# A fused scan and feed-forward kernel on one core: a fifth weight-ring entry, a transpose table, new step tables, and even pairs of row 0 summed on TensorE

## What is computed

```python
xx, res = split(x @ in_w.T, 2)                  # 512 inner channels each
xx = silu(conv4(xx) + conv_b)                   # causal, per channel
delta, B, C = split(xproj(xx), [16, 32])
delta = softplus(delta @ dt_w.T + dt_b)
for l in range(512):                            # 16 states per channel
    h = exp(delta[l] * A) * h + delta[l] * B[l] * xx[l]
    y[l] = sum over states of h * C[l]
y = (y + xx * D) * silu(res)
x = layernorm(x + y @ out_w.T)
h = silu(x @ w1.T * s1) * (x @ w2.T * s2)       # 1024 hidden
h = gelu(h @ h1.T * s); h = gelu(h @ h2.T * s)  # 1024 x 1024 each
out = layernorm(x + h @ w3.T * s3)
```

## Time and profile before

| | |
|---|---|
| median of 3 runs | 2764.91 us (2760.35 to 2766.14) |
| the profiled execution's own time | 2763.87 us |
| its span, first to last instruction | 2762.0 us |
| busy share of the span | PE 88%, DVE 86%, ACT 77%, POOL 62% |
| share of the 16 DMA engines' span, two main queues | 52.3% (GpSimd's), 33.5% (SP's) |
| mean granted TensorE clock | 0.947 |

### The profile page before, as it was taken

The page is one execution under the profiler, slowest core; times in us unless marked ns, Lnnn a source line. Parts: engine busy times, 40 slices in busy tenths (PEclk is TensorE's granted clock), DMA queues, the critical chain, the costliest instruction groups (busy, mean ns, idle before and its releaser), DMA issues. The chain is left out here.

```text
span 2762.0 us, 36137 instructions
## 1 busy us (share of the span) xinstructions
PE 2432.1 (88%) x12034; PEld 1844.0 (67%) x12034; DVE 2386.9 (86%) x2356; ACT 2114.3 (77%) x3225; POOL 1708.1 (62%) x1607
## 2 busy tenths in 40 slices
PE   5567998989899898989989899998989999898988
PEld 2335675767767576776757677675766767576767
DVE  6788899999999989999999999999898999989730
ACT  5676887969788796978879697887969789696711
POOL 1345666765665676566667656666765676666644
PEclk6568999999999999999999999999999999999999
DMA  5988898989989898998979889898988989898933
GB/s 164 312 207 192 204 227 197 241 194 219 219 207 229 194 241 200 216 221 206 229 194 239 201 214 219 206 228 195 241 203 211 216 208 226 203 232 204 252 95 118
DMA packets 226794, 581.64 MB, mean 211 GB/s; under 512 B 25920, under 2 KB 26304, under 8 KB 226128
## 3 DMA queue, kind: packets, MB, share of 16 engines
q0 software_dynamic: 73728, 268.47, 52.3%
q1 hardware_dynamic: 152880, 310.84, 33.5%
HBM read 301.86 MB, written 20.45 MB: 117 GB/s over the span
## 5 line engine op out<-in xcount | busy, mean ns | idle before, releaser
L767 DVE TENSOR_TENSOR_SCAN scan_ps<-dA,scan_ps 128x1024 f32<-128x1024 f32 x381 | 870.9, 2286 | 113.7 <-PE scan_ps L402 106.4
L626 ACT ACTIVATE dB<-duT,bT 128x512 f32<-128x512 f32 x1024 | 715.4, 712 | 115.5 <-PE scan_ps L402 115.5
L969 POOL DMA_DIRECT2D y<-hC x512 | 449.8, 879 | 543.4 <-DVE hC L778 382.6
L617 ACT ACTIVATE dA<-delta,a_neg 128x512 f32<-128x512 f32 (+1 forms) x1024 | 692.5, 711 | 3.1 <-DVE scan_ps L767 2.0
L402 PE MATMUL scan_ps<-ident,dB 128*128 128x128 f32 x4096 | 575.0, 287 | 130.6 <-DVE hC L778 107.5
L514 PE MATMUL ffn_ps<-hb_hi,ring 128*128 128x512 f32 x1536 | 649.7, 423 | 44.0 <-POOL hb_lo L1008 20.8
L402 PEld LDWEIGHTS scan_ps<-ident,dB 128*128 128x128 f32 x4096 | 500.1, 147 | 240.5 <-DVE hC L778 94.5
L514 PE MATMUL ffn_ps<-hb_lo,ring 128*128 128x512 f32 x1536 | 606.8, 395 | 0.0
L778 DVE TENSOR_TENSOR hC<-scan_ps,c_rows_sb 128x1024 f32<-128x1024 f32 x381 | 464.0, 1218 | 40.3 <-DMA c_rows_sb<-c_rows 11.0
L514 PE MATMUL ffn_ps<-ha_hi,ring 128*128 128x512 f32 x1024 | 437.8, 428 | 6.3 <-POOL ha_lo L1008 4.6
L961 POOL TENSOR_TENSOR hC<-hC,c_rows_sb 128x1024 f32<-128x1024 f32 x131 | 324.5, 2477 | 183.4 <-DVE hC L767 179.4
(11 more groups left out here) (99 smaller groups left out, 3168.5 us busy)
## 6 DMA issues: line engine op xcount, KB each, us to landing
y<-hC POOLq DMA_DIRECT2D x512, 512.0 KB, 6.0
ring<-rounded_weights SPq DMA_DIRECT2D x704, 256.0 KB, 4.1
c_rows_sb<-c_rows SPq DMA_DIRECT2D x256, 256.0 KB, 4.7
x<-ffn_w SPq DMA_DIRECT2D x22, 512.0 KB, 8.1
rounded_weights<-ffn_w SPq DMA_DIRECT2D x22, 512.0 KB, 10.3
xt<-x_chan SPq DMA_DIRECT2D x16, 512.0 KB, 4.2
xt<-x_tok SPq DMA_DIRECT2D x16, 512.0 KB, 4.4
out_st<-x_chan SPq DMA_DIRECT2D x16, 512.0 KB, 4.6
```

The source lines that it names most:

```text
L617: nc.scalar.activation(dA[:, s % DA_RING, s % 2:], delta2[:, par, c, s % 2:], ACT.Exp, scale=a_neg[:, c, n:n + 1]).then_inc(dA_ready, 1)
L626: nc.scalar.activation(dB[:, n % 2, t, :], duT[:, t, :], ACT.Copy, scale=bT2[:, par, t, n:n + 1]).then_inc(dB_ready, 1)
L767: nc.vector.tensor_tensor_scan(states, dA[:, a:a + 2, :].rearrange("p a l -> p (a l)"), b, 0.0, ALU.mult, ALU.add).then_inc(scan_done, 1)
L969: pool.dma_start(y2[:, par, c:c + 2, :], hC[:, slot], accum_op=ALU.add).then_inc(y_added[p % 2], 16)
```

## The change

- The ring has five entries, and an entry's place goes by its number over all rows (44 is no multiple of 5). To make room, small tables are computed in place of their inputs. The next row's first five entries are loaded in step 18, not four in step 14.
- `b_pair` goes by a table `B_AT`: within some steps of where it stood.
- Most step tables are laid anew. `POOL_PAIRS` has six pairs, not eight; `FIRST_POOL_PAIRS` (row 0) is as it was.
- Row 0 adds its 16 even pairs on TensorE (`sum_pair`: two products with the identity into `ffn_ps[1]` and `ffn_ps[2]`, which are free in iteration 0), and VectorE adds the two sums to `y2` in step 0 of iteration 1. Its 16 even transfers are gone.
- The DRAM copy of the weights is issued ten slots before row 0's scan and twelve during it, every fifth step.

```diff
-RING = 4
+RING = 5
-T_RES = (0, 4, 5, 8)
-T_GATE = (2, 5, 7, 11)
-T_OUT = (12, 13, 14, 17)
-T_ADD = (15, 18)
+T_RES = (0, 6, 7, 9)
+T_GATE = (2, 5, 8, 11)
+T_OUT = (12, 14, 16, 17)
+T_ADD = (16, 18)
-E_W3 = (10, 11, 13, 14)
-E_SCALE = (12, 17)
-E_ADD = (14, 19)
-E_STATS = (15, 21)
+E_W3 = (10, 11, 12, 18)
+E_SCALE = (12, 19)
+E_ADD = (14, 20)
+E_STATS = (17, 21)
-L1_AT = (22, 23, 24, 25, 26, 27, 28, 29)
-HALF_AT = (31, 32, 34, 35, 36, 38, 40, 41, 42, 43, 45, 46, 47, 48, 49, 50, 51, 52, 53, 54, 55, 57, 59, 60, 62,
-           63, 64, 65, 66, 68, 69, 71)
-GELU_AT = (38, 39, 39, 46, 46, 47, 50, 51, 55, 57, 57, 65, 66, 67, 71, 71)
+B_AT = (-2, 0, 4, 5, 7, 9, 10, 12, 14, 15, 18, 20, 22, 24, 26, 28, 31, 32, 34, 35, 37, 40, 42, 43, 47, 48, 50, 51,
+        54, 56, 58, 61)
+L1_AT = (22, 24, 25, 26, 27, 28, 29, 31)
+HALF_AT = (31, 32, 34, 35, 36, 37, 38, 40, 42, 44, 45, 46, 47, 48, 49, 50, 51, 52, 53, 54, 55, 56, 57, 60, 61, 62,
+           63, 64, 65, 70, 71, 72)
+GELU_AT = (38, 39, 39, 45, 46, 47, 49, 51, 56, 57, 57, 65, 65, 66, 72, 72)
-F_DT = (40, 41, 43, 44)
-F_PLUS = (45, 46, 48, 50)
-F_BASE = (40, 41, 43, 46)
-F_LOST = (46, 49, 51, 52)
-F_LN = 52
+F_DT = (40, 41, 43, 46)
+F_PLUS = (44, 46, 47, 49)
+F_BASE = (41, 43, 46, 50)
+F_LOST = (47, 47, 49, 51)
+F_LN = 51
-COPY_AT = tuple(range(6, 2 * SLOTS + 6, 2))
+COPY_AT = tuple(range(-26, -16)) + tuple(range(2, 62, 5))
+CLOSE_AT = 0
-POOL_PAIRS = (0, 8, 10, 12, 13, 16, 17, 28)
+POOL_PAIRS = (1, 8, 11, 13, 16, 17)
 FIRST_POOL_PAIRS = (0, 3, 4, 9, 14, 16, 17, 18, 25, 27, 28)
+SUM_AT = tuple(min(63, 2 * p + (5 if p in FIRST_POOL_PAIRS else 3)) for p in range(0, PAIRS, 2))
...
+            def sum_pair(p):
+                wait_product(pe, 0, p)
+                for c in range(2):
+                    mm = nc.tensor.matmul(ffn_ps[1 + c][:], ident[:], hC[:, p % HC_SLOTS, c, :],
+                                          start=(p == 0), stop=(p == PAIRS - 2))
+                mm.then_inc(y_summed, 1)
...
-                    if s % 2 == 0:
-                        if s // 2 + 1 < PAIRS:
-                            if scan is not None:
-                                b_pair(scan, s // 2 + 1)
-                        elif front is not None:
-                            b_pair(front, 0)
+                    if scan is not None and s in B_AT:
+                        b_pair(scan, B_AT.index(s))
+                    if front is not None and s - TILES in B_AT:
+                        b_pair(front, B_AT.index(s - TILES))
+                    if i == 0 and s in SUM_AT:
+                        sum_pair(2 * SUM_AT.index(s))
...
+                    if i == 1 and s == CLOSE_AT:
+                        dve.wait_ge(y_summed, PAIRS // 2)
+                        for c in range(2):
+                            nc.vector.tensor_tensor(y2[:, 0, c, :], ffn_ps[1 + c][:], y2[:, 0, c, :], ALU.add
+                                                    ).then_inc(y_closed, 1)
...
+                if on_pe(r, p):
+                    return
                 wait_product(pool, r, p)
```

More of the change, by code:

```diff
@@ L62 @@
 F_DBL_OUT = 40
-F_BT = 46
+F_BT = 48
 F_BT_OUT = 51
-F_DT = (40, 41, 43, 44)
-F_PLUS = (45, 46, 48, 50)
-F_BASE = (40, 41, 43, 46)
-F_LOST = (46, 49, 51, 52)
-F_LN = 52
+F_DT = (40, 41, 43, 46)
[3 more added lines that the diff above has]
+F_LN = 51
 F_DELTA = (53, 53, 53, 53)
 F_DELTA_U = (53, 53, 53, 53)
-F_Y = (55, 55, 58, 63)
-F_DU = (54, 55, 56, 58)
+F_Y = (59, 59, 61, 63)
+F_DU = (55, 56, 57, 58)
 F_XR = 51
@@ L104, in products_upto, with added_upto, on_pe @@
     return sum(on_pool(k // PAIRS, k % PAIRS) == pool for k in range(r * PAIRS + p))
+def added_upto(r, p, k):
+    return 16 * sum(q % 2 == k and not on_pe(row, q) for row in range(r + 1) for q in range(p if row == r else PAIRS))
+def on_pe(r, p):
+    return r == 0 and p % 2 == 0
 def build(nc, x, xT_in, in_wT, chan, xproj_wT, dt_wT, out_wT, ffn_w, ffn_s, w3_s, ident_in, out):
@@ L162, in build @@
         rstd = sb("rstd", [P, 2, TT])
+        conv_half, a_neg = ch[:, :, 0:TAPS + 1], ch[:, :, C_ALOG:]
+        s1_half, s12_half = fs[:, 0, :], fs[:, 1, :]
         xT_front = xt[:].rearrange("p (k t) d -> p k (t d)", k=KD)
@@ L262, in wait_slot @@
             g = r * PAIRS + p - HC_SLOTS
-            if g >= 0:
-                eng.wait_ge(y_added[g % 2], 16 * (g // 2 + 1))
+            if g >= 0 and on_pe(g // PAIRS, g % PAIRS):
+                eng.wait_ge(y_summed, g // 2 + 1)
+            elif g >= 0:
+                eng.wait_ge(y_added[g % 2], added_upto(g // PAIRS, g % PAIRS + 1, g % 2))
         def main_loop(eng, iteration, *args):
@@ L342, in load_weights @@
                         sp.wait_ge(pe_half, f * HALVES + (used - FIRST_HALF + 1))
-                    dst = ring[:, e % RING, :].bitcast(F32)
+                    g = f * ENTRIES + e
+                    dst = ring[:, g % RING, :].bitcast(F32)
                     src = w_dram[e // 2]
                     sp.dma_start(dst, src[:, (e % 2) * ENTRY_COLS:(e % 2 + 1) * ENTRY_COLS]
-                                 ).then_inc(ring_loaded[e % RING], 16)
+                                 ).then_inc(ring_loaded[g % RING], 16)
             def iteration(i, par):
@@ L351, in iteration @@
                 for s in range(TILES):
-                    if (s + 4) % DC == 0:
-                        n = (s + 4) // DC
+                    if (s + C_LEAD) % DC == 0:
+                        n = (s + C_LEAD) // DC
                         if n < STATES:
@@ L501, in wait_entry, with entry @@
             def wait_entry(f, e):
-                per_row = ENTRIES // RING
-                pe.wait_ge(ring_loaded[e % RING], f * (16 * per_row) + 16 * (e // RING + 1))
-            def entry(e):
-                return ring[:, e % RING, :]
+                g = f * ENTRIES + e
+                pe.wait_ge(ring_loaded[g % RING], 16 * (g // RING + 1))
+            def entry(f, e):
+                return ring[:, (f * ENTRIES + e) % RING, :]
             def products(dst, steps, first, last, full):
@@ L526, in l1_tile @@
                         pe.wait_ge(l1_x32 if prev % 2 else l1_gate, f * HC + (prev // 2 + 1))
-                    steps = [(entry(o)[:, (q * KD + k) * P:(q * KD + k + 1) * P], a[:, k, :])
+                    steps = [(entry(f, o)[:, (q * KD + k) * P:(q * KD + k + 1) * P], a[:, k, :])
                              for k in range(KD) for a in (x1T_hi, x1T_lo)]
@@ L545, in half_tile @@
                 wait_entry(f, e)
-                steps = [(entry(e)[:, k * P:(k + 1) * P], a[:, kh * HC // 2 + k, :])
+                steps = [(entry(f, e)[:, k * P:(k + 1) * P], a[:, kh * HC // 2 + k, :])
                          for k in range(HC // 2) for a in src]
@@ L560, in w3_tile @@
                         wait_entry(f, e)
-                    steps = [(a[:, 2 * q + k, t * P:(t + 1) * P], entry(e)[:, k * DIM:(k + 1) * DIM])
+                    steps = [(a[:, 2 * q + k, t * P:(t + 1) * P], entry(f, e)[:, k * DIM:(k + 1) * DIM])
                              for k in range(2) for a in (ha_hi, ha_lo)]
@@ L982, in gate_tile @@
                     for k in range(2):
-                        pool.wait_ge(y_added[k], r * (8 * PAIRS) + 8 * PAIRS)
+                        wait_past(pool, y_added[k], added_upto(r, PAIRS, k))
+                    if r == 0:
+                        pool.wait_ge(y_closed, 2)
                 pool.wait_ge(v_ready, r * DC + (c + 1))
```

32 lines of the change are left out of this document (15 added, 17 removed).

## The result

The changed kernel takes 2681.82 us (median of 4 runs, 2681.34 to 2685.69), the kernel before in the same series 2765.52 us. The ratio is 0.9701, interval 0.9685 to 0.9716: 3% faster. The profiled execution's span went from 2762.0 to 2679.5 us, 82.5 us less. 2714 us was predicted, with 2675 to 2762 as the range. The direction and the range held; the gain is 82.5 us in the span where 50.2 were summed.

What follows compares the result with a forecast made beforehand. A round was taken as a long part TensorE ends and a short one VectorE ends. Gains of 37.7 (13 rounds), 8 (row 0), 1.5 (row 1) and 3 (end), together 50.2 us, gave 2714 us, range 2675 to 2762.

Steps and rivals of the forecast that it cites:

- The serial piece: Half tiles reordered around step 39's `xproj` product: 2.2 us a round saved before scans 22 to 24, 0.3 wait at 21.
- Gate: Gates early in a round: 1.9 us tanh wait becomes 1.0, the next vanishes; 1.2 of waiting at pair 2's transposes.
- The end of the long part: Before pair 9's transposes: TensorE work moves to idle time, ending waits of 0.65 us before scan 9 and 0.7 for `hb_hi`.
- Products on VectorE: Two pairs' products a round move from GpSimd to VectorE: 2.4 us charged, bounds 1.2 to 2.4.
- The sum of a round: Steady round: 5.3 of 10.8 us of VectorE waits saved, 2.4 paid, 2.9 gained; 37.7 over 13 rounds.
- The ring: Ring entry loads held to step 18: no gain, no cost; if late, one landing (4 us) a round.
- Row 0: Sums replace 16 transfers: 12 us of transfer waits saved, 4 of new transpose waits, 8 gained (-3 to 14).
- Row 1, last row and drain: Row 1 gains 1.5 us after 1.4 for closing the sums; drain gains 2, the last row's scans 1.
- Transfers bind: Rival, chance 0.12: the stretch with transfer share 1.00 keeps its length, so 1.0 us a round gained; 2740 us.
- TensorE binds row 0: Rival, chance 0.12: at the lower clock the sums fill TensorE; row 0 loses 5 us instead of gaining 8; 2727 us.
- Nearly all waits go: Rival, chance 0.07: nearly all VectorE waits in a round vanish, 8.4 us a round gained; 2637 us.
- Slower: Rival, chance 0.11: saved waits return at the next transposes and two products lengthen VectorE's part, 34 us lost; 2787 us.

Runs made afterwards that it cites:

- The serial piece alone: Kernel before with five half tiles moved around the `xproj` and `dt` products as in the change, nothing else: 2775.30 us, ratio 1.0040.
- The late W3 tile alone: Kernel before with only the fourth `w3_tile` moved behind the output products (step 14 to 18, its scaling and addition later): 2748.88 us, ratio 0.9947.
- single products: Kernel before with one GpSimd product given to VectorE, in two runs: pair 28 2776.18 us (ratio 1.0047), pair 12 2778.77 us (1.0050).
- the old eight pairs: Changed kernel with GpSimd's products set back to pairs 0, 8, 10, 12, 13, 16, 17, 28: 2729.18 us, ratio 0.9876.
- the ring of four: Changed kernel with four ring entries in place of five, all else as changed: 2765.64 us, ratio 0.9997.

## Why the prediction was right, and where it was mis-sized

**What bounds the kernel: right in kind.** A round ends by hand-overs between TensorE and VectorE, and the waits of VectorE that the experiments on the order of work moved could be named. But the walk left out one side of these hand-overs, as the ring and the GpSimd pairs show.

**The serial piece: right.** Expected 1.5, 0, 1.5 and 0.3 us before scans 22, 23, 24 and 21; measured 1.51, none, 0.78, 0.44. The serial piece alone in the kernel before gave the first two and 2.56 at pair 24. So the other tables fill 1.8 us of that gap, which fits the 1.3 to 2.2 credited to `F_PLUS` and `F_LOST`; no run isolates these two.

**Gate: right in kind.** Expected 1.0 for tanh and 1.2 at pair 2; measured 0.9 and 0.8. The 0.9 are two waits, so the second one shrank and did not vanish.

**The end of the long part: right.** The wait before scan 9 and that for `hb_hi` are gone. The late W3 tile alone takes the first away, and leaves 0.6 us a round of the second.

**Products on VectorE: the pairs were taken for work alone.** 2.4 us were charged. In the kernel before, single products cost 0.8 and 1.1, so as a price of the work the charge was fair. In the changed kernel busy time rose by 1.8 a round, and the old eight pairs cost 3.3 us a round rather than saving 2.4. The step counted what VectorE has to do and did not walk what the choice sets for the transposes two pairs on: a pair on GpSimd frees its bank of `scan_ps` at the end of its scan, a pair on VectorE only at the end of its product. With pair 11 on GpSimd the transposes of pair 13 need not wait, and both runs that gave pair 11 back and pair 10 to GpSimd lose 2.5 us a round there.

**The sum of a round: low.** 2.9 predicted, 4.5 measured. Over the 13 rounds VectorE's named waits went from 11.3 to 4.6 us, 6.7 saved where 5.3 were counted (1.4), and its busy time rose by 1.8 rather than 2.4 (0.6); its other idle time rose by 0.4.

**The ring: the step that failed.** "No gain, no cost" was read from the kernel before, where landings of 4.1 us came in time, and where four entries suffice even with the late W3 tile. With the new pairs SP's queue stops behind pair 11's product, and without the fifth entry the whole gain is lost. The prediction named the price of a late load (4 us a round, 6.2 measured) but not what makes it late: it did not follow the C load of pair 11's buffer, which stands ahead of the entries on SP, to the GpSimd product that frees it. The term of nothing came out right only because the change brought both together, and that is luck. What a fifth entry does in the kernel before was not run; with 3.7 us of ring waits in all there is little for it to take away.

**Row 0: mis-sized.** 8 predicted, 15.7 measured. Waits for transfers fell by 9.7 us where 12 were taken. The sums ended at 35.7 us of TensorE, near the lower price of 30 rather than 57, since they raised the clock themselves; new waits for transposes were nil (3.4 before, 3.2 after) where 4 were set. Not in the sum were 3.5 us less of waits for ScalarE's `y` and 2.7 less of busy time. The copies' place can't be told from nothing.

**Row 1, last row and drain.** Row 1 gained 1.6 for 1.5, from a round that was 4.5 shorter and not 2.9, so the agreement may be luck: it takes 154.8 us without the closing additions, and 154.6 to 155.7 in the kernels that have them and the changed table of the transposes, so that their price isn't told from nothing. The last row and the drain gave 5.9 for 3. From its first to its last scan the last row took 144.1 us before and 143.8 after, so its scans gave 0.3 and not 1, and 5.6 come behind them. The gap in the drain shrank by 2.3 as walked; the rest was not followed.

**The rivals.** Transfers bind: wrong. From scan 26 of row 9 to scan 4 of row 10 the transfer share is 1.00 in both kernels, and this stretch went from 47.5 to 44.7 us. TensorE binds row 0: wrong, 96.3 us busy of 136.2. Nearly all waits go: not reached, 4.6 of 11.3 us are left. Slower: in the changed kernel the waits didn't change place. Alone in the kernel before, the new order of half tiles did just that (3.5 us won and 3.5 lost), while the late W3 tile kept 0.9 of its 1.4. So the mechanism is real, and the tables together escape it.

## What to carry to other kernels

Walk through each engine's written order with durations from the trace: where the new order was walked, waits came out to 0.1 to 0.7 us. But a table of steps is not a sum of its entries: test a part both alone in the old kernel and missing from the new one. Here products handed to VectorE cost 0.8 and 1.1 us a round in the old kernel, and handing two back cost 3.3 in the new one. When a piece of work moves to another engine, ask what buffer its end frees and who waits for that. And before a queue's depth is called free, look at what stands ahead of its loads in the issuing engine's order, and which engine frees that.

## What the runs showed of the hardware

Five ring loads of 256 KB, issued one behind another after a stop of the queue, took a median of 8.4 us to land in the ring of four (1546.2 to 1560 us), beside 4.1 us over the kernel before. The 16 sums in row 0 (32 products of 128x512) raised its granted clock from 0.62 in the kernel without them to 0.83, and the transposes there take 320 ns each, where they took 389 at 0.59 before the change. A 128x512 scaling on VectorE takes 0.48 us with GpSimd at rest, and up to 1.54 us when it starts beside a GpSimd product or split: it then ends 0.27 to 0.29 us after that instruction (all 38 cases over 0.6 us before and after).
